# A two-layer AdaLN transformer: the first attention's output projection in three passes behind the query product, and layer 1's modulation blocks loaded in routing

## The reference

```python
mod = (silu(L0_c) @ L0_wmod).reshape(1, 6, 1, -1)     # shift, scale, gate, twice
h = layernorm(x) * (1 + ca) + sa
x = x + ga * L0_attn(h)          # 16 heads of 32, 2 key-value groups, overlapping windows of 64 keys
h = layernorm(x) * (1 + cb) + sb
x = x + gb * L0_ffn(h)           # 64 experts, 8 of them for each token
mod = (silu(L1_c) @ L1_wmod).reshape(1, 6, 1, -1)
x = x + ga * L1_attn(...)        # 16 heads, 4 key-value heads, sliding window of 128 with 16 meta keys
x = x + gb * L1_ffn(...)         # Hadamard transforms around a gated block of 2048
```

## Time and profile before

| | us |
|---|---|
| median of 3 runs | 2128.39 |
| lowest and highest of them | 2127.51, 2128.79 |
| the profiled execution's own time | 2135.61 |
| its span | 2133.4 |
| its first attention, to the first routing product | 0 to 291.7 |
| its routing, to the first expert product | 291.7 to 368.4 |

### The profile page before, as it was taken

How to read it: one execution, slowest core, us unless ns; L and a number is a source line. 1 busy time by engine, 2 the same in 40 slices (tenths; PEclk the granted TensorE clock), 3 DMA queues, 4 the chain that set the end, 5 groups by cost and what they waited for, 6 DMA issues and landing times. The chain is left out here.

```text
span 2133.4 us, 38655 instructions
## 1 busy us (share of the span) xinstructions
PE 1975.7 (93%) x11379; PEld 1338.6 (63%) x11381; DVE 1033.5 (48%) x3280; ACT 756.1 (35%) x1770; POOL 734.8 (34%) x668
## 2 busy tenths in 40 slices
PE   6899867999999999999999489999889999999998
PEld 4667644555555555555555267777668878788786
DVE  3577667344555322222222487887644543443432
ACT  1233227222222222222222167787733323232222
POOL 1344310454555554545455364554301011011000
PEclk9999889999999999999999699999999999999999
DMA  9113442698878889988888311100121121121210
GB/s 334 45 66 106 158 127 78 165 232 207 193 179 196 202 212 234 226 206 198 199 234 206 88 34 35 35 4 6 59 91 68 60 79 60 69 69 59 81 67 20
DMA packets 111020, 265.95 MB, mean 125 GB/s; under 512 B 25792, under 2 KB 29504, under 8 KB 110784
## 3 DMA queue, kind: packets, MB, share of 16 engines
q1 hardware_dynamic: 66336, 164.36, 23.5%
q0 software_dynamic: 35552, 88.63, 20.5%
q10 hardware_dynamic: 9024, 11.54, 1.5%
HBM read 200.22 MB, written 63.21 MB: 123 GB/s over the span
## 5 line engine op out<-in xcount | busy, mean ns | idle before, releaser
L1294 PE MATMUL bank<-arena 128*128 x1272 | 439.7, 489 | 1.5 <-ACT arena L1335 0.9
L1247 POOL DMA_INDIRECT x_sum<-route,arena x158 | 254.3, 1609 | 182.2 <-DVE route L1421 157.9
L1294 PEld LDWEIGHTS bank<-arena 128*128 128x128 f32 x1272 | 229.9, 191 | 131.9 <-issue 6.3
L1311 PE MATMUL bank<-arena 96*128 x632 | 299.8, 596 | 4.4 <-issue 3.9
L1258 POOL DMA_INDIRECT arena<-h_moe,arena x158 | 155.7, 985 | 227.1 <-DVE arena L1415 218.0
L1408 DVE SCALAR_TENSOR_TENSOR arena<-arena,bank 128x192 f32<-128x192 f32 x159 | 65.9, 415 | 312.2 <-ACT arena L1330 311.6
L2125 PE MATMUL bank<-x_hi,w_hi 128*128 128x512 f32 x512 | 201.5, 394 | 6.0 <-DVE x_lo L2256 6.0
L2125 PE MATMUL bank<-x_lo,w_hi 128*128 128x512 f32 x512 | 203.2, 397 | 0.0
L2125 PE MATMUL bank<-x_hi,w_lo 128*128 128x512 f32 x512 | 202.1, 395 | 0.0
L1330 ACT ACTIVATE arena<-bank 128x192 f32<-128x192 f32 x159 | 52.7, 331 | 352.7 <-PE bank L1294 352.7
L1311 PEld LDWEIGHTS bank<-arena 96*128 96x128 f32 x632 | 107.3, 190 | 85.3 <-issue 84.7
(11 more groups left out here) (366 smaller groups left out, 3648.7 us busy)
## 6 DMA issues: line engine op xcount, KB each, us to landing
arena<-in_moe_up SPq DMA_DIRECT2D x64, 768.0 KB, 6.1
ffn_arena<-in_ffn_up SPq DMA_DIRECT2D x61, 512.0 KB, 3.2
arena<-in_moe_down SPq DMA_DIRECT2D x64, 384.0 KB, 7.6
arena<-in_L_wmod SPq DMA_DIRECT2D x12, 1024.0 KB, 7.2
x_sum<-route SPq DMA_DIRECT2D x18, 256.0 KB, 3.5
x_res<-in_L_attn_x SPq DMA_DIRECT2D x1, 4096.0 KB, 28.7
h_moe<-arena SPq DMA_DIRECT2D x16, 256.0 KB, 2.2
x_sum<-x_res SPq DMA_DIRECT2D x16, 256.0 KB, 2.6
```

The costliest lines, as they stand in the source:

```text
L1247: nc.gpsimd.indirect_dma_start(out=x_sum[b], out_offset=bass.IndirectOffsetOnAxis(ap=st_dst[:, b], axis=0), in_=y[:, b], in_offset=None, c ...
L1294: mm = nc.tensor.matmul(psum[2 + b][:, 0:2 * FI], xgT[:, b, k], up_ring[:, bass.ds((e % RING) * UPW + k * 2 * FI, 2 * FI)], start=(k == 0) ...
L1311: mm = nc.tensor.matmul(psum[6 + b][:], hiddenT[:, b, n], down_ring[:, bass.ds((e % RING) * DOWNW + n * C, C)], start=(n == 0), stop=(n == 1))
```

## The change

1. From tile w = 4 on (`PLAIN = 4`) the output projection is done with rounded operands (type float32r, FR): a high part of oT and of wo and the rest of each. Three products for each of the four slices of 128: high x high, high x rest, rest x high, so 12 matmuls of 128x512. Tiles 0 to 3 keep the four f32 products.
2. ScalarE's copy of oT now makes the high part. VectorE makes the rest (`rest_of`), placed between the first subtraction of scores and the third maximum. ScalarE makes wo's high part in turn 3 (four copies), VectorE its rest behind turn 4 (`wo_rest`, four subtractions).
3. For all tiles the output projection stands elsewhere in TensorE's list: in turns with a block f behind the query product, in the others behind the transposes of the probabilities.
4. The new buffers take the room of `routed.wm`. So the three loads of layer 1's modulation blocks leave the attention and stand at the start of SyncE's list in routing, ahead of the loads of the first three experts.

```diff
@@ -158,6 +158,12 @@
+        with ExitStack() as opening:
+            room = lambda name, dtype, *shape: opening.enter_context(nc.sbuf_tensor(name, [P, *shape], dtype))[:]
+            room("attn0_gap", F32, FT * C + TEND)
+            wo0_hi, wo0_lo = room("wo0_hi", FR, KC, C), room("wo0_lo", FR, KC, C)
+            oT0_hi, oT0_lo = room("oT0_hi", FR, KC, P), room("oT0_lo", FR, KC, P)
@@ -302,7 +308,9 @@
+            PLAIN = 4
@@ -377,9 +384,6 @@
-                        if s >= NT - 2 - WMB and s < NT - 2:
-                            sp.wait_ge(mod_mm, 6)
-                            sp.dma_start(routed.wm[:, s - (NT - 2 - WMB)], wmods[s - (NT - 2 - WMB)]).then_inc(wm_in, 16)
@@ -456,7 +459,13 @@
-                        nc.scalar.copy(oT.rearrange("p k n -> p (k n)"), tp[:]).then_inc(oT_out, 1)
+                        to = oT if w < PLAIN else oT0_hi
+                        nc.scalar.copy(to.rearrange("p k n -> p (k n)"), tp[:]).then_inc(oT_out, 1)
+                    if w == PLAIN - 3:
+                        act.wait_ge(ready, 2)
+                        act.wait_ge(mod_mm, 6)
+                        for k in range(KC):
+                            nc.scalar.copy(wo0_hi[:, k], wo[:, k]).then_inc(wo_hi_done, 1)
@@ -505,6 +514,19 @@
+                def out_product(w):
+                    pe.wait_ge(oT_out, w + 1)
+                    if w < PLAIN:
+                        pe.wait_ge(ready, 2)
+                        passes = [(oT[:, k], wo[:, k]) for k in range(KC)]
+                    else:
+                        pe.wait_ge(wo_lo_done, KC)
+                        pe.wait_ge(oT_lo_out, w - PLAIN + 1)
+                        passes = [(x[:, k], y[:, k]) for k in range(KC) for x, y in ((oT0_hi, wo0_hi), (oT0_hi, wo0_lo), (oT0_lo, wo0_hi))]
+                    for n, (x, y) in enumerate(passes):
+                        mm = nc.tensor.matmul(tp[:], x, y, start=(n == 0), stop=(n == len(passes) - 1))
+                    mm.then_inc(wo_mm, 1)
@@ -542,12 +564,6 @@
-                    if w is not None:
-                        pe.wait_ge(oT_out, w + 1)
-                        pe.wait_ge(ready, 2)
-                        for k in range(KC):
-                            mm = nc.tensor.matmul(tp[:], oT[:, k], wo[:, k], start=(k == 0), stop=(k == KC - 1))
-                        mm.then_inc(wo_mm, 1)
@@ -556,6 +572,8 @@
                         mm.then_inc(q_mm, 1)
+                    if f is not None and w is not None:
+                        out_product(w)
                     if s is not None:
                         pe.wait_ge(p_sub, HP * s + HP)
@@ -575,6 +593,8 @@
                                 mm.then_inc(pT_mm, 1)
+                    if f is None and w is not None:
+                        out_product(w)
@@ -649,6 +669,17 @@
+                def rest_of(w):
+                    if w >= PLAIN:
+                        dve.wait_ge(oT_out, w + 1)
+                        nc.vector.tensor_tensor(oT0_lo.rearrange("p k n -> p (k n)"), tp[:], oT0_hi.bitcast(F32).rearrange("p k n -> p (k n)"),
+                                                ALU.subtract).then_inc(oT_lo_out, 1)
+
+                def wo_rest():
+                    dve.wait_ge(wo_hi_done, KC)
+                    for k in range(KC):
+                        nc.vector.tensor_tensor(wo0_lo[:, k], wo[:, k], wo0_hi[:, k].bitcast(F32), ALU.subtract).then_inc(wo_lo_done, 1)
@@ -748,6 +779,8 @@
                         for r in range(HP + 1):
+                            if r == 2 and w is not None:
+                                rest_of(w)
@@ -757,6 +790,8 @@
+                    elif w is not None:
+                        rest_of(w)
@@ -816,6 +851,8 @@
+                    elif m == 4:
+                        wo_rest()
@@ -881,10 +919,12 @@
                 sp.dma_start(cols, a["c_cols"][:, 1]).then_inc(c_in, 16)
+                w = a["L1_wmod"].rearrange("(k p) (j n) -> j p k n", p=P, j=6)
+                for j in range(WMB):
+                    sp.dma_start(routed.wm[:, j], w[j]).then_inc(wm_first, 16)
                 for e in range(AHEAD):
@@ -954,7 +994,9 @@
-                        if j >= WMB:
+                        if j < WMB:
+                            pe.wait_ge(wm_first, 16 * WMB)
+                        else:
                             pe.wait_ge(wm_in[j - WMB], 16)
```

More of the change, by code:

```diff
@@ L160, in adaln_two_layers @@
         ffn_scales = sb("ffn_scales", [P, 3, FT])
+        with ExitStack() as opening:
[3 more added lines that the diff above has]
+            oT0_hi, oT0_lo = room("oT0_hi", FR, KC, P), room("oT0_lo", FR, KC, P)
+        assert 2 * KC * C + 2 * KC * P + 8 <= WMB * KC * C
         scoped = ctx.enter_context(ExitStack())
@@ L304, in adaln_two_layers @@
             x_in = psem("a_x_in")
-            sim_in, wm_in, wd_in = psem("a_sim_in"), psem("a_wm_in"), psem("a_wd_in")
+            sim_in, wd_in = psem("a_sim_in"), psem("a_wd_in")
+            wo_hi_done, wo_lo_done, oT_lo_out = psem("a_wo_hi_done"), psem("a_wo_lo_done"), psem("a_oT_lo_out")
+            PLAIN = 4
             N_DMA, N_DMA2 = 8, 3
@@ L361, in _ @@
                     sp.dma_start(routed.sim[E * r:E * r + E], a["L0_ffn_similarity"]).then_inc(sim_in, 16)
-                wmods = a["L1_wmod"].rearrange("(k p) (j n) -> j p k n", p=P, j=6)
                 zero = routed.zeros
@@ L394, in _ @@
                 sp.wait_ge(x_kept, 16 * NT)
-                sp.wait_ge(wm_in, 16 * WMB)
                 sp.wait_ge(wd_in, 16)
@@ L876, in adaln_two_layers @@
             wm_in = [psem(f"r_wm_in{j}") for j in range(WMB)]
+            wm_first = psem("r_wm_first")
             HAD0 = 4
@@ L886, in _ @@
                     sp.dma_start(arena[0:FH, down_at(e):down_at(e) + DOWNW], a["moe_down"][e].rearrange("p k n -> p (k n)")).then_inc(ahead_in, 16)
-                w = a["L1_wmod"].rearrange("(k p) (j n) -> j p k n", p=P, j=6)
                 sp.dma_start(routed.su_row, a["L1_ffn_SU_ug"].partition_broadcast(P)).then_inc(rows_in, 16)
```

## The result

The changed kernel takes 2155.75 us (median of 4 runs, 2149.0 to 2160.55). The kernel before, run beside it, takes 2127.95 us (4 runs, 2127.49 to 2128.79). The ratio is 1.0115, with a 95% interval of [1.0096, 1.0133], so the change costs some 24.5 us; the two medians lie 27.8 us apart, inside that interval. In a later comparison it was 1.0119 [1.0096, 1.0142], with medians of 2156.65 and 2134.47 us. The forecast was 2150 us and +22. Four executions of all that are told of here lie far outside the rest (2342.87 to 5135.58 us), and every ratio and median goes by the others.

What follows compares the result with a forecast made beforehand. TensorE's own list was taken to bound each turn. Terms of +12.9 us at an unchanged clock and +9 for the clock made +22 on the 2128.4 median: 2150 us, own range 2142 to 2162, 8 in 10 2132 to 2169.

Steps and rivals of the forecast that it cites:

- Odd turns: First attention, split tiles w = 5 to 13: TensorE idles 3.1 us for VectorE's subtractions; +1.70 us each, +8.5 in all.
- plain turn 5: Odd turns with plain f32 tiles, w = 1 and 3: the same wait without the rest, +1.75 us each, +3.5 in all.
- VectorE's wait for the copy of oT: Odd turns: ScalarE's copy ends at 190.68, VectorE arrives at 190.70, so no wait before the rest, which takes 0.69 us.
- Even turns: Query product first, waiting for ScalarE's copy: -0.3 us for each of five split turns, -1.5; plain w = 0, 2: +1.0.
- Once: Behind turn 4: VectorE's four subtractions for wo's rest stand ahead of o, for which TensorE waits; +2.5 us.
- The last two turns: Turns 16 and 17 of the attention: -1.7 and +0.6 us, together -1.1, or -3 if the clock is full.
- Transfers: Three 1 MB loads moved to routing: 3.1 MB at 275 GB/s take about 11.5 us, 7 us to spare; cost 0.
- The clock: TensorE's granted clock falls in all seven odd turns, five of them new, 1.8 us each: +9 us.
- rival 2: The clock stays low longer, in seven odd and seven even turns: +40.6 us, 2169 us; chance 0.13.
- Rival 1: The waits come but the clock falls no more often than before: +12.9, 2141 us; chance 0.16.
- Rival 3: VectorE's part is not late, waits under 0.8 us, dense passes pay in full: faster, 2119 us; chance 0.08.
- rival 4: No difference: waits cost 13 us, passes win back the 10.9 us lost to low clock: +2, 2130 us; chance 0.08.

Runs made afterwards that it cites:

- e5: The changed kernel plus three unused f32 products of 128x512 ahead of TensorE's wait for the subtractions in odd turns: 2145.0 us, ratio 1.0055 to the kernel before.
- e9: e6 with four f32 products for all tiles, no split, no `wo_rest` and no use of the other bank: 2141.74 us, ratio 1.0040 to the kernel before.
- e4: The kernel before with only the three modulation loads moved from the attention to routing: 2135.05 us against 2134.13, ratio 1.0006.
- e6: Changed kernel with odd-turn projection ahead of the wait, in bank 6, high-part passes first, `wo_rest()` inside turn 4: 2127.06 us against 2134.13 for the kernel before.
- e2: The changed kernel with the odd turns' projection put back ahead of the wait for VectorE's subtractions: 2138.22 us, ratio 1.0026 to the kernel before.

## Why the prediction was right

**Odd turns.** The mechanism, the wait's name and its length came as forecast: 3.06 us in split turns (3.1), with 2.44 without the rest. With the clock taken out, the part of a turn that lengthened did so by 1.64 us (e5's turn), and 1.70 was forecast. In the plain turn 5 the transposes of the probabilities start 117.51 - 114.41 = 3.10 us behind those of o. With 0.88 and 3.53 us behind them at full clock that makes 7.51, +1.76 against the earlier trace rows; 1.75 was forecast:

```profile
114.41 0.65 PE L555 MATMUL bank<-ident,arena 128*128 128x128 f32 x4 [3.04 <-DVE arena L765]
117.51 1.97 PE L592 MATMUL bank<-ident,mod 128*128 128x128 f32 x8 [2.45 <-DVE mod L791]
119.27 5.02 PE L527 MATMUL bank<-arena 128*128 128x512 f32 x8
```

**VectorE's wait for the copy of oT.** I said that there would be none. It is 0.37 us in turn 9, which comes to its transposes at the low clock; the other four split odd turns have none:

```profile
176.78 1.11 PE L555 MATMUL bank<-ident,arena 128*128 128x128 f32 x4 [0.64 <-DVE arena L765]
```

```profile
178.55 0.69 DVE L675 TENSOR_TENSOR oT_lo<-bank,oT_hi 128x512 fp32r<-128x512 f32 x1 [0.37 <-ACT oT_hi L463]
```

The transposes of o take 1.11 us there and not 0.66, so ScalarE's copy is late. The gap in the rows of before was 0.02 us wide, too thin to call it no wait. The rest itself took the 0.69 us of the earlier trace rows.

**Even turns.** -0.2 us each, against -0.3: the wait for ScalarE's copy is 0.73 us, and the first pass takes 0.32 to the next and not 0.23. In f32 the later start costs 0.48, as e9 shows.

**Once.** Turn 5's transposes of o wait 3.04 us in the row above and start 3.95 us into the turn, against 1.54 in turn 11: +2.41, forecast 2.5. The last two turns (from the transposes of o of turn 16 to routing) take 36.76 us instead of 37.41, -0.65 against -1.1. That this came near is luck: turn 16 is 2.21 us shorter (-1.7 forecast) because its passes ran at full clock, 2.98 us and not the 4.9 assumed, and turn 17 is 1.56 longer (+0.6 forecast), since its wait for o is 3.59 us instead of 1.95.

**Transfers.** 0, as forecast (e4). My reason was sound but its rate was too low: 395 GB/s instead of the 275 of the earlier trace rows. As an estimate from that rate, and from the 94 GB/s of the stage's first 2.75 us, the 3.1 MB are in at about 327 us, 9 before the product starts at 336.12.

**The clock.** This is the term that was mis-sized: "five are new: 5 x 1.8 = +9 us". The other terms, with the measured sizes, add up to 8.2 + 3.5 - 1.0 + 1.0 + 2.4 - 0.65 = 13.5 us (12.9 forecast). The attention lost 25.55, which leaves 12 for the clock. A count by turns agrees. From the transposes of the probabilities to those of h2 the seven odd turns lose 1.43, 2.20, 2.42, 2.86, 1.68, 2.75 and 2.62 us against full clock, 16.0 in all. A slow query product in turn 6 and slow passes in turn 14 add 1.8 and 1.7. (A slow query product in turn 2, 1.7 us, is left out of the count, and so are the slow transposes of turn 14 before, 1.6 us; they cancel.) Of the earlier trace rows's 10.9 us, 6.4 lay in these turns before (4.5 in the last two projections, 255.62 and 269.09), so 19.5 - 6.4 = 13.1. After's second trace, whose attention is 1.8 us shorter, leaves 10 by the first way. So the term is 10 to 13 us where I had 9. Two things I had wrong here. The loss in an odd turn is 2.3 us on average and not 1.8, because the eight transposes behind the wait are slow as well (1.97 us instead of 1.04). And some even turns behind them lose too, as rival 2 had it, though in two of seven (6 and 14). The reading that the wait brings the clock down holds for the sum, as e5 shows, but not for each turn: in turn 9 it was down before.

Rival 1 (clock no worse) falls with the 16.0 us of slow work in the odd turns, where 4.2 stood before, and with e5. Rival 3 needed a wait of under 0.8 us, and rival 4 passes that win back the clock; the rows show neither. Waits that short in split odd turns stand only where the passes come ahead of the wait in another order (e6) or unused work fills it (0.48 us in e5).

## What to carry to other kernels

Before a product is moved behind a semaphore wait, look at what it covered at its old place: here 3.5 us of product hid VectorE's subtractions, and no saving in the product could replace that cover. Price an idle gap of TensorE twice, once for itself and once for the work behind it that runs at the low clock. Where a product of high parts and rests waits for the rests, put the passes that need only high parts first, in a bank that is free, and let the passes fill the wait.

## What the runs showed of the hardware

- Work whose results nobody reads makes the changed kernel faster (though not as fast as the one before): three f32 products in each odd turn's idle time brought the 60 to 280 us stretch from a granted clock of 0.85 to 0.94 and routing forward by 12.6 us (e5, 12.8 us by the ratios).
- The granted clock has no fixed place to fall at around a wait of 3.1 us: in turn 11 it is 1.00 in the window without any work of TensorE, 0.72 in the next and 0.50 in the one after, in turn 7 it falls to 0.71 and 0.50 while TensorE has no work, and in turn 9 it is down before the wait.
- At the low clock a pass of 128x512 takes 0.43 us to its successor and at the full one 0.23; four f32 products are 3.60 to 3.70 us long at full clock and up to 6.76 where it is low for most of them.
- The same program scatters by its clock: in e2 two executions at 0.959 and 0.967 took 2150.93 and 2130.88 us. Small terms (under 3 us) can't be read from one pair of traces: turn 4 of the kernel after took 16.57 us in one trace and 19.39 in the other.
